# A message-passing layer whose node rows are gathered by two queues: 17 tiles instead of 12 go row by row through SyncE's queue

## The reference

```python
h = jnp.maximum(_layernorm(x), 0.0)
s, v = h[:, :64] @ W_nl0, einsum('nmi,mk->nki', h[:, 64:], W_nl1)   # one table row of 160 for a node
w = relu(edge_attr_64 @ W_fc1) @ W_fc2                              # 224 weights for each edge
xs, xv = s[dst], v[dst]                                             # gather of table rows, one for each edge
tp = concatenate([w0*xs, w3*dot(xv, sh1), (w1*xs)*sh1, w2*xv, w4*cross(xv, sh1)])
agg = segment_sum(tp, src, N) / 32                                  # scatter-add by the other end
out = x + gated(agg @ W_out + skip)
```

## Time and profile before

| | us |
|---|---|
| median of 3 runs | 1391.45 (1389.9 to 1393.38) |
| the profiled execution, its own time | 1393.36 |
| its span | 1391.5 |

### The profile page before, as it was taken

The page is one execution under the profiler, slowest core; times in us unless marked ns, Lnnn a source line. Parts: engine busy times, 40 slices in busy tenths (PEclk is TensorE's granted clock), DMA queues, the critical chain, the costliest instruction groups (busy, mean ns, idle before and its releaser), DMA issues.

```text
span 1391.5 us, 26137 instructions
## 1 busy us (share of the span) xinstructions
PE 938.8 (67%) x5702; PEld 797.2 (57%) x5702; DVE 877.6 (63%) x3681; ACT 433.9 (31%) x849; POOL 1067.2 (77%) x830
## 2 busy tenths in 40 slices
PE   8499675775766858657677577675776767759203
PEld 5287564664655746546566566574765656648202
DVE  7599765756656667476575675766757657568205
ACT  5254232232332323323323223232332322324201
POOL 1577888888887887888878888888788888887880
PEclk9799787788786877777868678787787777878656
DMA  9534455545454555445555555555555555455557
GB/s 346 156 87 107 82 103 78 106 81 80 105 80 82 103 80 105 79 81 103 80 99 87 80 105 80 91 94 80 105 79 83 104 78 105 79 79 87 52 53 277
DMA packets 120683, 139.76 MB, mean 100 GB/s; under 512 B 31105, under 2 KB 96449, under 8 KB 120578
## 3 DMA queue, kind: packets, MB, share of 16 engines
q0 software_dynamic: 79296, 74.04, 37.4%
q1 hardware_dynamic: 41282, 64.79, 15.1%
HBM read 86.10 MB, written 52.66 MB: 100 GB/s over the span
## 4 chain that ended last, share of the span: by engine, by line
DMA 30%; POOL 26%; DVE 23%; issue 13%; PE 5%; DVEq 2%; POOLq 0%; SPq 0%; ACT 0%
DMA sums<-to_add,add_idx 14%; DMA sums<-spare,add_idx 14%; POOL turn_space L376 9%; POOL sums L394 8%; DVE products_space L763 6%; POOL rows L376 5%; POOL spare L376 5%; DVE products_space L792 4%; DVE before L831 2%; DVE same L830 2%; DVE products_space L790 2%; DVE products_space L789 2%; DVE radial L805 1%; DVE msg L816 1%; DVE turn_space L774 1%
## 5 line engine op out<-in xcount | busy, mean ns | idle before, releaser
L481 PE MATMUL t_ps<-w,products_space 128*128 128x128 f32 (+1 forms) x1248 | 227.5, 314 | 341.8 <-DVE products_space L792 341.7
L497 PEld LDWEIGHTS o_ps<-w,pT 128*128 128x128 f32 (+1 forms) x2496 | 369.6, 228 | 40.7 <-issue 37.8
L497 PE MATMUL o_ps<-w,pT 128*128 128x96 f32 (+1 forms) x2496 | 385.6, 314 | 0.0
L394 POOL DMA_INDIRECT sums<-to_add,add_idx x208 | 328.6, 1580 | 66.5 <-issue 46.0
L481 PEld LDWEIGHTS t_ps<-w,products_space 128*128 128x128 f32 (+1 forms) x1248 | 169.2, 162 | 363.2 <-issue 327.2
L394 POOL DMA_INDIRECT sums<-spare,add_idx x208 | 326.9, 1572 | 63.8 <-issue 46.7
L604 ACT ACTIVATE pT<-t_ps 128x512 f32<-128x512 f32 (+1 forms) x312 | 185.3, 594 | 315.5 <-PE t_ps L481 315.2
L855 DVE TENSOR_TENSOR add_idx<-key,from_col 128x4 int32<-128x4 f32 x104 | 17.0, 164 | 362.3 <-DMA sums<-spare,add_idx 197.9
L376 POOL DMA_INDIRECT turn_space<-node_table,to_idx x186 | 187.0, 1005 | 56.7 <-issue 46.9
L613 ACT ACTIVATE msg<-o_ps 128x448 f32<-128x448 f32 x208 | 113.0, 543 | 346.3 <-PE o_ps L497 334.4
L512 PE MATMUL d_ps<-msg,same 128*128 128x192 f32 x832 | 197.1, 365 | 25.1 <-ACT spare L625 14.1
(11 more groups left out here) (93 smaller groups left out, 898.9 us busy)
## 6 DMA issues: line engine op xcount, KB each, us to landing
from_row<-nodes_row SPq DMA_DIRECT2D x52, 512.0 KB
ef<-edge_t SPq DMA_DIRECT2D x52, 256.0 KB
turn_space<-node_table SPq DMA_DIRECT2D x768, 0.6 KB
spare<-node_table SPq DMA_DIRECT2D x768, 0.6 KB
turn_space<-sums SPq DMA_DIRECT2D x9, 480.0 KB, 5.7
sums<-zeros SPq DMA_DIRECT2D x6, 672.0 KB, 8.8
sums<-to_add,add_idx POOLq DMA_INDIRECT x208, 3.6
sums<-spare,add_idx POOLq DMA_INDIRECT x208, 3.6
```

The lines of the kernel that those rows point to most:

```text
L394: pool.indirect_dma_start(sums[t], bass.IndirectOffsetOnAxis(ap=add_idx[:, 2 * v + h, j:j + 1], axis=0), to_add[2 * v + h][:, j, :], None, ...
L481: ins = nc.tensor.transpose(t_ps[(3 * u + c) % 2][0:ROWS[c], j * P:(j + 1) * P], prod[:, u % 2, j, a:e], ident)
L497: ins = nc.tensor.matmul(o_ps[m][:, base + oc:base + oc + n], pT[c][u % 2][:, cols], w[0:ROWS[c], wc:wc + n], start=(q == 0 and c == 0), s ...
```

## The change: what it does

`BY_ROW_SLOTS` becomes (5, 10, 15). The groups whose last tile goes row by row are then 15, 21, 26, 31, 37, 42, ... 95, 101: seventeen instead of twelve. POOL issues 399 gathers instead of 404. `ROWS_PER_BLOCK` goes from 32 to 48, so a pass of SP issues 48 row DMAs after three register loads instead of 32 after two, until the 2176 rows are done, in pass 45 (before: 1536 rows, pass 47). As 128 is no multiple of 48, a pass may end one tile and begin the next, so the loop looks up group and row for every 16 rows. The node numbers of the tiles lie on 17 partitions of 128 numbers each, and no longer in one row of 1536.

```diff
-BY_ROW_SLOTS = (7, 15)
+BY_ROW_SLOTS = (5, 10, 15)
...
-        by_row_idx = sb("by_row_idx", [1, len(BY_ROW) * P], I32)
+        by_row_idx = sb("by_row_idx", [len(BY_ROW), P], I32)
...
             def gather_rows(b):
 
-                k, r0 = divmod(b * ROWS_PER_BLOCK, P)
-                if k >= len(BY_ROW):
-                    return
-                g = BY_ROW[k]
-                u = g % ROWS_RING
-                if r0 == 0 and valid(g - ROWS_RING, GROUPS):
-                    sp.wait_ge(prod_ready, 2 * (g - ROWS_RING) + 2)
-                for r in range(r0, r0 + ROWS_PER_BLOCK, ROWS_PER_LOAD):
+                for first in range(b * ROWS_PER_BLOCK, (b + 1) * ROWS_PER_BLOCK, ROWS_PER_LOAD):
+                    k, r = divmod(first, P)
+                    if k >= len(BY_ROW):
+                        return
+                    g = BY_ROW[k]
+                    u = g % ROWS_RING
+                    if r == 0 and valid(g - ROWS_RING, GROUPS):
+                        sp.wait_ge(prod_ready, 2 * (g - ROWS_RING) + 2)
                     _, nodes = nc.values_load_multi_w_load_instructions(
-                        by_row_idx[0:1, k * P + r:k * P + r + ROWS_PER_LOAD], engines=[mybir.EngineType.SP],
+                        by_row_idx[k:k + 1, r:r + ROWS_PER_LOAD], engines=[mybir.EngineType.SP],
...
-        "nodes_by_row": np.ascontiguousarray(in_blocks(dst)[[g * J + BY_ROW_J for g in BY_ROW], :, 0].reshape(1, -1)),
+        "nodes_by_row": np.ascontiguousarray(in_blocks(dst)[[g * J + BY_ROW_J for g in BY_ROW], :, 0]),
```

## The result

The changed kernel takes 1405.24 us at the median (1404.72 to 1428.9, 6 runs), the kernel before 1391.87 in the same sets (6 runs). The ratio is 1.0093, with an interval of 1.0082 to 1.0105: 13 us slower. By the ratio the 1391.45 us of then become 1404.4, at the upper edge of the range: the direction and the place were right, the size was short by 5 us.

The account below looks back on a forecast made before the run. POOL's own issuing was taken as the bound, passing to SP's longer pass after the change. 6.4 us gained by gathers and 14.4 lost against loads gave +8.0: from 1391.45 to 1399.5 us, range 1384.5 to 1405.

Parts of the forecast that it names:

- POOL sets the end, and five gathers are worth 6.4 us: On POOL: its own issuing sets the end; five gathers less, at 1.27 us each, gain 6.4 us.
- The pass grows to 25.45 us and SP stops waiting: On SP: a pass grows from 17.48 to 25.45 us, 0.48 us over POOL's 24.97 us block, so SP never waits.
- The rival that hung on it: SP's register loads at the 0.6 us floor: pass 23.6 us, SP waits again, plain gain to 1385; chance 0.22.
- Lateness of `ef` and `from_row` costs nothing: On PE and DVE: loads up to 31 us late cost 0, as `add_idx` is made some 100 us ahead.
- The loads drift into the scatter-adds, and the drift stops itself: SP's loads drift 0.48 us a pass into POOL's scatter-adds, until POOL loses about 0.48 us a block at SP's pace.
- Where they lock: `from_row` settles 1.5 us ahead of the block's first scatter-add; block 42 starts scattering at 1193.6, 8.0 us later.
- The drain is as before: Blocks 43 to 51, after SP's last rows in pass 45: DVE catches up and nothing changes.
- What the profile after would show: SP passes 25.4 to 25.5 us without L278 waits; POOL's landing gaps 0.5 to 2 us, summing to ten or more.
- the loss against the loads: POOL's scatter-adds delayed by SP's loads up to block 42: 14.4 us lost.

Follow-up runs that it names:

- the spread loads: Changed kernel with `from_row` loaded in two 256 KB halves between portions of rows, `ef` ahead of them: 1393.41 us, ratio 1.0003 to the kernel before.
- the two slow chips: Changed kernel with `from_col` on ACT, with 32 numbers a register load (twice), or both, on chips slowing the kernel before too: 1590.52, 1672.69, 1714.03, 1655.19 us.
- the loads on ACT: Changed kernel with `from_col`, `from_row` and `ef` issued by ACT instead of SP: 1423.2 us, ratio 1.0224 to the kernel before.
- The long pass with 12 tiles: Kernel before with one more register load and 16 more DMAs of 4 bytes in each SP pass that issues rows: 1400.72 us, ratio 1.0062.

## Why the prediction was right, and where its sizes were off

*POOL sets the end, and five gathers are worth 6.4 us.* Shown: with the loads in their old place the kernel with 399 gathers is 7 us faster. (That kernel brings 48 rows of each of the seventeen tiles in one DMA, so it shows what the gathers are worth and not that it can be had.)

*The pass grows to 25.45 us and SP stops waiting.* Measured 25.53 us. The register load from another partition takes 1.24 us at the median, as before (1.22), so the change of layout costs nothing, and the floor of 0.6 us that the Trainium skill gives ("DMA: Bandwidth & Descriptors", Latency and other measured facts) is half of what this kernel's loads take. The rival that hung on it fell by the same number. But 0.08 us a pass over 43 passes is 3.4 us: pass 45 began at 1195.3 and not at 1191.7. This is the first mis-sized term. The 25.45 held up to pass 19, with 25.42; the excess came afterwards, with 25.60, once the loads stood among the scatter-adds. Its register loads were 1.23 us at the median up to there and 1.26 after, which with three a pass is nearly half of it; the rest I can't name.

*Lateness of `ef` and `from_row` costs nothing.* Shown by the spread loads, where SP is later and the kernel faster, though PE's 398 us of waiting for `ef` look grave. Where the bound lies, some 100 us by the forecast, no run measured; POOL's waits of up to 15 us for ACT appear only on the two slow chips.

*The loads drift into the scatter-adds, and the drift stops itself.* Shown: up to block 16 the loads stand ahead and a block takes 25.11 us, behind it 25.61 as SP's pass; cutting the burst gives 12 of 13 us back; and with the loads on ACT every block with `from_row` behind the first scatter-add has its wait and no block with it ahead. The long pass with 12 tiles (8 us) shows something else, which the forecast had put at nothing: a load that comes close costs through longer issues before any landing is late. In the changed kernel that ate the gathers' gain in blocks 2 to 16 already, where 25.11 us stand against the 24.97 forecast.

*Where they lock.* I took 1.5 us ahead of the first scatter-add; it is 0.5 us behind it in block 41 and level in block 42, and it became steady after some 17 passes and not ten. This is the second mis-sized term, of the opposite sign: block 42 began at 1195.69, 10.1 us later than in the earlier trace rows, forecast were 8.0.

*The drain is as before.* This was wrong, by 3.2 us: from block 42 to 44 it took 1248.57 - 1195.69 = 52.9 us, before 49.7. SP had run out of rows in pass 45 and made up its delay, so that four passes' loads went out within two blocks, three of them beside scatter-adds. In POOL's timeline of block 42, with SP's `from_row` at 1195.70 and 1204.98:

```profile
1202.16 1.56 POOL L394 DMA_INDIRECT sums<-spare,add_idx  x1 [0.76 <-DMA sums<-spare,add_idx]
...
1210.50 1.55 POOL L394 DMA_INDIRECT sums<-spare,add_idx  x1 [1.20 <-DMA sums<-spare,add_idx]
```

Two hits in one block. The sum as measured on the profiled executions: +10.1 up to block 42, +3.2 to block 44, -1.1 behind it, 12.2 us.

*What the profile after would show.* Right were the passes, the waits at L278, the gaps that name a landing, and DVE, which now waits 329 us for PE and hardly for scatter-adds. Right was also their sum, "ten or more us". POOL's waits for landings:

```profile
POOL sums L394 <- DMA sums<-to_add,add_idx: 24.9, 52, 2.0
POOL sums L394 <- DMA sums<-spare,add_idx: 23.0, 51, 1.7
```

From these 47.9 us the usual 0.30 in 103 cases has to be taken: 17.0 us, where before it was 34.4 less 108 times 0.30, 2.0 us.

*What the sum lacked.* Between blocks 2 and 42 the kernel after took 1017.4 us, the one before 1005.4, 12.1 us more (it began block 2 2.0 us earlier, which gives the +10.1). The waits for landings are 11.0 us of that. The scatter-adds' issues are another 5.8 (508.4 for 502.6), and the gathers' 1.7 (305 took 307.2, at the old mean 305.5). Against them stand five gathers less, 6.5. So the loss against the loads was 18.5 us in this stretch, with 14.4 forecast up to block 42, and 7.5 of it came by longer issues, for which the sum had no term. The forecast did not suffer by that, since in the lock SP's pass sets the time however the loss is made up; in this it was lucky. What left it 4.2 us short on the profiled executions are 3.6 us by the passes and 2.1 by the drain and the end, less 1.5 by the lock.

## What to carry to other kernels

A queue that issues transfers for others has a deadline in each round of the kernel: once its own round is longer than that of the engine that sets the pace, it no longer waits, and everything it loads loses its place. Before giving such a queue more work, compare its round with the pacing engine's and not with its idle share; here 7.6 us a pass were free (25.12 - 17.48; the 8.3 of the earlier trace rows is a mean that the long waits at both ends raise), 8.0 were added, the round of the pacing engine was itself to shrink by 0.15, and that half microsecond too much cost three times what the offload won. What it costs is decided by the largest burst and by what that burst then lies beside, so cutting the burst or keeping the wait that places it can matter more than issue time.

## What the runs showed of the hardware that was not expected

- A register load of 10 node numbers took 1.82 us at the median (1.13 to 2.78), one of 16 numbers 1.22 to 1.24 us. Less is not cheaper; 32 took 2.2 us on the two slow chips.
- The issue of an indirect scatter-add on POOL is not constant. Beside load transfers it took 1.76 instead of 1.56 us; the mean over 416 was 1.572 us with all loads beside gathers and 1.598 with loads spread over the block.
- A scatter-add's own data moved only after its issue was over. In the kernel before, the packets of a block's first scatter-add began 2.2 us after the start of its issue, which takes 1.6 us, and scatter-adds landed after 3.6 us at the median. With 768 KB of loads issued 0.85 us behind it they began after 3.6 us (block 32 of the kernel after).
- On two chips single instructions of SyncE took 0.7 us and more again and again in the four kernels traced there: 64 row DMAs took 45.2 us where 29 are expected. These kernels took 160 to 253 us more than the kernel before beside them, and that one 39 to 69 us more than in the first set.
